# Masked MLP: transposes of the down product two groups ahead on three buffers, and search steps placed by duration

## The reference

```
x = x + attention(layernorm(x))          # 32 heads of 16, causal
x = x + ffn(layernorm(x))                # "f1"
x = x + masked_mlp(layernorm(x))         # "gates" and "down"
x = x + ffn(layernorm(x))                # "f2", same weights as f1

ffn:        down(silu(x @ gate) * (x @ up))         # 1792 wide, int weights dequantised
masked_mlp: s = silu(x @ w_gate.T)                  # 1376 wide
            s[the 688 smallest |s| of each row] = 0 # top_k(-abs(s), 688)
            (s * (x @ w_up.T)) @ w_down.T
```

## Time and profile before

| | us |
|---|---|
| median of three timed runs | 2203.8 |
| lowest and highest of them | 2194.07, 2206.63 |
| the profiled execution, its own time | 2189.01 |
| its span in the profile | 2187.2 |
| mean granted TensorE clock in it | 0.97 |

### The profile page before, as it was taken

How to read it: one execution, slowest core, us unless ns; L and a number is a source line. 1 busy time by engine, 2 the same in 40 slices (tenths; PEclk the granted TensorE clock), 3 DMA queues, 4 the chain that set the end, 5 groups by cost and what they waited for, 6 DMA issues and landing times.

```text
span 2187.2 us, 38402 instructions
## 1 busy us (share of the span) xinstructions
PE 2021.1 (92%) x14288; PEld 1234.7 (56%) x14288; DVE 1543.5 (71%) x2736; ACT 1022.0 (47%) x1658; POOL 558.7 (26%) x587
## 2 busy tenths in 40 slices
PE   5887999999999887899999999999999979889989
PEld 2342344444444345677677677677677555556656
DVE  6775677777777341289688597696696898989841
ACT  3221456656566521265364364373463564646511
POOL 2224354644342241012112012012012111121221
PEclk9997899999999988999999999999999999999999
DMA  7766234533233072110310400500400403031000
GB/s 258 236 220 175 67 99 117 139 88 83 76 84 93 19 244 110 55 50 1 108 49 1 154 23 1 175 1 1 174 2 14 152 1 132 24 113 53 11 11 10
DMA packets 115656, 187.35 MB, mean 86 GB/s; under 512 B 43200, under 2 KB 68176, under 8 KB 115520
## 3 DMA queue, kind: packets, MB, share of 16 engines
q1 hardware_dynamic: 91344, 133.22, 19.6%
q0 software_dynamic: 9088, 32.12, 5.1%
q10 hardware_dynamic: 15088, 20.19, 2.6%
HBM read 151.59 MB, written 33.62 MB: 85 GB/s over the span
## 4 chain that ended last, share of the span: by engine, by line
PE 46%; DVE 12%; issue 3%; ACT 1%; POOL 0%; DVEq 0%; ACTq 0%; POOLq 0%
PE ga L1364 10%; PE acc L1374 10%; PE ub L1364 10%; DVE junk L1534 7%; PE ga L1392 5%; PE ub L1392 5%; PE acc L1417 4%; DVE pat L1538 2%; DVE h L1591 1%; PE d_tr L1213 1%; DVE T L1540 1%; DVE lohi L1606 1%; PE d_tr L1403 0%; DVE X L1616 0%; DVE d_xn L1200 0%
## 5 line engine op out<-in xcount | busy, mean ns | idle before, releaser
L842 DVE TENSOR_REDUCE mx<-s 128x1 f32<-128x512 f32 (+3 forms) x608 | 380.8, 661 | 125.7 <-PE s L731 72.3
L1465 ACT ACTIVATE junk_a<-ax,T 128x1376 f16<-128x1376 f32 x248 | 357.8, 1443 | 200.8 <-DVE T L1540 195.1
L823 ACT ACTIVATE pr<-s 128x1024 f32<-128x1024 f32 (+3 forms) x352 | 301.2, 869 | 240.3 <-PE s L750 178.4
L1534 DVE TENSOR_SCALAR_CACHE_REDUCE junk<-ax,T 128x1376 f16<-128x1376 f32 x248 | 406.8, 1640 | 3.5
L1326 POOL TENSOR_TENSOR lohi<-h,lohi 128x256 f16<-128x256 f32 x224 | 172.7, 771 | 871.9 <-ACT lohi L1476 871.5
L1364 PE MATMUL ga<-xT_f,w_gate 128*128 128x256 f16 x2688 | 336.3, 276 | 38.4 <-DVE h L1591 35.3
L1364 PE MATMUL ub<-xT_f,w_up 128*128 128x256 f16 x2688 | 333.1, 274 | 0.0
L1364 PEld LDWEIGHTS ga<-xT_f,w_gate 128*128 128x128 f16 x2688 | 261.8, 99 | 121.1 <-DVE h L1591 54.7
L1374 PE MATMUL acc<-w_down,lohi 128*128 128x512 f16 x1344 | 326.1, 379 | 2.8 <-DVE X L1616 2.8
L1364 PEld LDWEIGHTS ub<-xT_f,w_up 128*128 128x128 f16 x2688 | 264.9, 99 | 32.4
L728 PE MATMUL s<-K,Q 65*128 65x512 f16 (+3 forms) x768 | 244.8, 344 | 26.0 <-DMA K<-onerow 12.9
(11 more groups left out here) (142 smaller groups left out, 2407.2 us busy)
## 6 DMA issues: line engine op xcount, KB each, us to landing
ring<-wgu_scr SPq DMA_DIRECT2D x64, 688.0 KB, 5.0
ring<-wd_scr SPq DMA_DIRECT2D x24, 768.0 KB, 4.7
wgu_scr<-tk_h POOLq DMA_DIRECT2D x16, 344.0 KB, 6.1
q_scr<-qk_h ACTq DMA_DIRECT2D x16, 256.0 KB, 4.0
k_scr<-qk_h ACTq DMA_DIRECT2D x16, 256.0 KB, 2.5
v_scr<-v_f ACTq DMA_DIRECT2D x16, 256.0 KB, 3.5
Q<-q_scr SPq DMA_DIRECT2D x32, 128.0 KB
K<-k_scr SPq DMA_DIRECT2D x32, 128.0 KB
```

What stands on the lines that cost most here:

```text
L823: nc.scalar.activation(pr[:, kb % 2, j0:j1, 0:w], scores, ACT.Exp, scale=SCALE).then_inc(e2_ok, 1)
L842: nc.vector.tensor_reduce(dst, s1[u % 2][:, 0:(j1 - j0) * w].rearrange("p (j k) -> p j k", k=w), AX.X, ALU.max).then_inc(r1_ok, 1)
L1465: nc.scalar.activation(junk_a[:, :], ax[k % 2][:, 1, :], ACT.Sign, scale=-1.0, bias=TF[:, 1:2], accum_out=cnt[:, 1:2]).then_inc(c1_ok, 1)
L1534: nc.vector.tensor_scalar(junk[:, :], ax[k % 2][:, 0, :], TF[:, 0:1], -float(KZERO), ALU.is_lt, ALU.add, accum_out=cnt[:, 0:1]).then_inc(c ...
```

## The change

Four edits, all in `phase_mlp` and `mlp_stages`:

1. `lohi` has NDT = 3 buffers in place of two; `hT` still uses the first two, `dT` all three. High and low halves and the product index `dT` by v % 3, and the high copy of group v waits for product v-3 in place of v-2.
2. TensorE's order in a down stage is turn 0, turn 1, then for each slot n: wait for low half n, turn n+2, product n. The wait for the low half stands ahead of turn n+2.
3. `junk_a` is removed. The sign pass writes its elementwise output into `kept[1]`, and the first sign pass of a chunk waits for both masks of the chunk before.
4. The items are placed by duration: `costs` gives each item its VectorE time, `evictions` and the terms beside it give VectorE's other work in a slot, and an item goes into a slot as long as the work done so far stays within the same share of all work as the time passed has of all time.

```diff
@@ phase_mlp @@
+    NDT = 3
...
-        lohi = [sb(f"lohi{i}", [P, 2 * DB * P], F16) for i in range(2)]
-        hT = [b[:, 0:2 * CW].rearrange("p (a n) -> p a n", a=2) for b in lohi]
+        lohi = [sb(f"lohi{i}", [P, 2 * DB * P], F16) for i in range(NDT)]
+        hT = [b[:, 0:2 * CW].rearrange("p (a n) -> p a n", a=2) for b in lohi[0:2]]
...
-        junk_a = sb("junk_a", [P, I_TK], F16)
...
@@ product_tk @@
-                pe.wait_ge(dl_ok, DU * k + v + 1)
...
-                        m = nc.tensor.matmul(acc[t][:, :], dT[v % 2][0:w, a, n, :], wr[:, b, :],
+                        m = nc.tensor.matmul(acc[t][:, :], dT[v % NDT][0:w, a, n, :], wr[:, b, :],
@@ TensorE's program @@
                     turn(s, 0)
+                    turn(s, 1)
                     if left:
...
-                        if n + 1 < DU:
-                            turn(s, n + 1)
+                        pe.wait_ge(dl_ok, DU * s.c + n + 1)
+                        if n + 2 < DU:
+                            turn(s, n + 2)
                         product_tk(s, n)
@@ signs, on ScalarE @@
                     act.wait_ge(t0_ok, k + 1)
+                    wait(act, hm_ok, TPC * k)
                 wait(act, p_ok, NBITS * k + i)
-                nc.scalar.activation(junk_a[:, :], ax[k % 2][:, 1, :], ACT.Sign, scale=-1.0, bias=TF[:, 1:2],
+                nc.scalar.activation(kept[1][:, :], ax[k % 2][:, 1, :], ACT.Sign, scale=-1.0, bias=TF[:, 1:2],
@@ turned, on ScalarE (turned_low on VectorE likewise indexes dT by v % NDT) @@
-                wait(act, dm_ok, DU * s.c + v - 1)
+                wait(act, dm_ok, DU * s.c + v - NDT + 1)
@@ mlp_stages @@
     spans = {"f1": 3860, "f2": 3860, "gates": 3460, "down": 1800}
+    evictions = {"f1": 430, "f2": 430, "gates": 530, "down": 460}
+    costs = [2450] * N_BITS + [80, 1740, 150, 950, 3180, 1650, 1900, 250, 250, 1740, 150, 150, 1740, 150, 950, 3180,
+                               1650, 1900]
     for k in range(NC):
         first = at["gates", k] + 1
-        own = [(slot, spans[s.kind]) for s in stages[first:at["down", k]] for slot in s.slots][:-2]
-        total = sum(span for _slot, span in own)
-        item = passed = 0
-        for slot, span in own:
+        own = [(slot, spans[s.kind], evictions[s.kind] + 700 * len(slot.taken) + 1800 * len(slot.stats)
+                + 1100 * len(slot.scaled) + 1400 * len(slot.lows))
+               for s in stages[first:at["down", k]] for slot in s.slots][:-2]
+        length = sum(span for _slot, span, _duty in own)
+        work = sum(duty for _slot, _span, duty in own) + sum(costs)
+        item = passed = done = 0
+        for slot, span, duty in own:
             passed += span
-            share = (N_BITS + FIN) * passed // total
-            slot.items += [(k, n) for n in range(item, share)]
-            item = share
+            done += duty
+            while item < len(costs) and (done + costs[item] // 2) * length <= passed * work:
+                slot.items.append((k, item))
+                done += costs[item]
+                item += 1
+        own[-1][0].items += [(k, n) for n in range(item, len(costs))]
     return stages
```

More of the change, by code:

```diff
@@ L1493, in turned @@
                     act.wait_ge(dn_ok, JB * s.ffns_done)
-                wait(act, dm_ok, DU * s.c + v - 1)
+                wait(act, dm_ok, DU * s.c + v - NDT + 1)
                 for rows, n0, n1_ in split_rows(v % DG):
-                    m = nc.scalar.activation(dT[v % 2][0:rows, 0, n0:n1_, :], tr[v % 2][0:rows, n0:n1_, :], ACT.Copy)
+                    m = nc.scalar.activation(dT[v % NDT][0:rows, 0, n0:n1_, :], tr[v % 2][0:rows, n0:n1_, :], ACT.Copy)
                     m.then_inc(dh_ok, 1)
@@ L1605, in turned_low @@
                 for rows, n0, n1_ in split_rows(v % DG):
-                    m = nc.vector.tensor_tensor(dT[v % 2][0:rows, 1, n0:n1_, :], tr[v % 2][0:rows, n0:n1_, :],
-                                                dT[v % 2][0:rows, 0, n0:n1_, :], ALU.subtract)
+                    m = nc.vector.tensor_tensor(dT[v % NDT][0:rows, 1, n0:n1_, :], tr[v % 2][0:rows, n0:n1_, :],
+                                                dT[v % NDT][0:rows, 0, n0:n1_, :], ALU.subtract)
                 m.then_inc(dl_ok, 1)
```

## The result

| | before | after |
|---|---|---|
| median of 13 runs, us | 2194.07 | 2182.07 |
| lowest and highest, us | 2186.63, 2207.63 | 2173.55, 2193.10 |
| span of the profiled execution, us | 2187.2 | 2172.5 |

The ratio of after to before is 0.9927, with a 95% interval of 0.9903 to 0.9951: the change makes the kernel 0.7% faster, 16 us of 2194 (11 to 21). The two medians are 12.0 us apart, which lies inside that interval too. The forecast was 15.8 us of 2189. As an absolute number it was 2188.0 us, 6 us above the median measured: with 13 runs in place of three, the median of the kernel before came down from 2203.8 to 2194.07.

What follows compares the result with a forecast made beforehand. TensorE bounds steady rounds; rounds of chunks 5 and 6 are bound by VectorE in one stage, TensorE in the next. Savings 2.0 + 5.9 + 3.7 + 4.2 = 15.8 us take 2203.8 to 2188.0 us, range 2172 to 2203.

Steps and rivals of the forecast that it cites:

- Part 1: Down stages: transposes two groups ahead leave the 1.62 us pause before product 0; net 0 per round.
- the slack: Between down slots, the new order gives VectorE one product more of room; credited with nothing.
- The mask wait: Downs 5 and 6: the first sign pass waits for GpSimd's mask, costing 1.1 us each, bounds 0 and 2.8.
- Round of chunk 5: Of VectorE's 11.9 us of waits 4.5 remain, 7.4 are saved; less 1.5 of collisions, net 5.9 us saved.
- The collisions of the pattern: Search's pattern instruction meeting GpSimd's low half takes 0.72 us, not 0.23; about 3 more in chunk 5's round, 1.5 us.
- Round of chunk 6: VectorE waits of 10.8 us, less 4.5 remaining, 1.5 of collisions and 1.1 of mask wait: 3.7 us saved.
- Round of chunk 7: TensorE's 5.9 us of waits for h and X go; down 6 costs 1.7; net 4.2 us saved.
- Round of chunk 0: TensorE's 2.0 us wait for X goes, as one step instead of two stands ahead of the addition.
- (a): Rival: VectorE's waits in rounds 5 and 6 reappear at down-stage ends and behind masks; 2197.6 us, chance 0.20.
- (b): Rival: the pause at each down start goes too, 11.3 us more saved; 2176.7 us, chance 0.05.
- (c): Rival: many pauses of about 1 us in f1 7 and f2 4 lower TensorE's clock; slower, 2229 us, chance 0.06.
- (d): Rival: nothing changes, as VectorE's total fixes the rounds and the rest is noise; 2203.8 us, chance 0.05.

Runs made afterwards that it cites:

- runs 5 to 7: The changed kernel with GpSimd's low half made to wait (2163.15 us), with a search step moved into the preceding down stage (2171.17), and with both (2170.66).
- run 5: The changed kernel with GpSimd's low half waiting, in slots holding only search steps, until the first step sets its next trial; 2163.15 us, ratio 0.9875.
- run 2: The kernel before with only the placement by duration; old order, two buffers and own scratch tile kept; 2179.34 us, ratio 0.9894.
- runs 1 and 2: The kernel before with everything but the new placement (2190.37 us, ratio 0.9953), and with the new placement alone (2179.34 us, 0.9894).
- Run 3: The kernel before with the new placement, old order, and the sign pass writing kept[1] behind the mask wait; 2175.17 us, ratio 0.9892.

## Why the prediction was right, point by point

**The bound.** Steady rounds bound by TensorE, rounds 5 and 6 by VectorE's work and idle time: runs 5 to 7 show it directly. The pattern instructions of these two rounds took 4.84 and 4.75 us more than their 0.229 us each in the changed kernel; with that gone in run 5 the rounds shortened by 4.8 and 4.7, and the steady ones kept their length.

**Part 1, costed at 0.** The pause of 1.62 us stayed, for the reason given. Off by size: a steady down lost 0.29 us. The trace of the kernel before shows where it stood. In a steady down the low halves of groups 5 and 7 each come right behind a search step:

```profile
1568.32 0.55 DVE L1606 TENSOR_TENSOR lohi<-d_tr,lohi 128x384 f16<-128x384 f32 x1
1568.46 0.49 PE L1403 MATMUL d_tr<-ident,pp 128*128 128x128 f32 x3
...
1568.93 2.12 PE L1417 MATMUL acc<-ring,lohi 128*128 128x512 f16 x9
...
1572.67 0.48 DVE L1606 TENSOR_TENSOR lohi<-d_tr,lohi 128x128 f16<-128x128 f32 x2
1573.20 0.98 PEld L1417 LDWEIGHTS acc<-ring,lohi 128*128 128x128 f16 x6 [0.48 <-DVE lohi L1606]
```

Product 5 starts 0.47 us after the transposes ahead of it, as its low half ends (1568.87), where 0.33 is usual. Product 7 loads its weights as its low half ends (1573.15), and the next stage starts 3.41 us after product 6 in place of the 3.24 of run 2. That is 0.14 + 0.17 us, each too short for a bracket on TensorE's matmuls. The order removes it because these groups are transposed one slot earlier, the placement because no step stands right ahead of these two; runs 1 and 2 agree. So the step that I had mis-sized is the slack: I gave nothing for it because where VectorE is late "it is the bound anyway", and it was late in steady downs too. In downs 4 to 6 the order gave 1.0 us in all where I gave nothing.

**The mask wait, 1.1 us twice.** Run 3 measured 0.79 and 0.78. The mechanism was the forecast one. In down 5 of the changed kernel VectorE took 2.1 us from the end of step 48 to its own first count, not 1.7: I had left out 0.53 us in which it waits for ScalarE's high copy of the group.

**Round of chunk 5, -5.9.** Down 4, f1 7 and gates 6 changed by -1.22 - 8.44 + 4.69 = -4.97 us. The gates' waits fell to 0, where I had left 0.5. Two things were mis-sized, and with them the sum comes to 4.7. The waits that remain are 5.0 us, not 4.5: the idle time at the first h is 3.87 us where I had 3.2, since VectorE is done earlier in the down stage but TensorE's last products and block 0 still follow. And a small instruction of the next layer norm met the new place of the first mask in gates 6, at 0.95 us where the same one took 0.17 on average before:

```profile
1814.91 2.79 POOL L1331 TENSOR_TENSOR pp<-pp,kept 128x1376 f32<-128x1376 f32 x1 [11.69 <-DVE kept L1586]
...
1816.79 0.95 DVE L1194 TENSOR_SCALAR rstd_f<-mv_f 128x2 f32<-128x2 f32 x1
```

The collisions of the pattern in this round were sized right. Its group from 1732.2 to 1804 us:

```profile
L1540 DVE TENSOR_SCALAR pat<-cnt,pow 128x2 int32<-128x2 f32 x25 | 10.6, 423 | 0.9
```

(10.6 - 25 x 0.229) / 0.49 = 10 of 25, three more than the 7 of before; in both traces the durations one by one give the same counts.

**Round of chunk 6, -3.7.** Measured -0.39 - 7.83 + 4.70 = -3.52.

**Round of chunk 7, -4.2.** The FFN stages lost 6.0 us against the 5.9 put down, down 6 gained 0.63 where I had 1.7. At 19.77 us it is 1.3 above the 18.46 of an undisturbed one, but the kernel before had lost 0.7 there already, which I had left out. Not foreseen was a loss at the end: TensorE waits twice for GpSimd's low halves.

```profile
2076.22 1.47 PE L1374 MATMUL acc<-w_down,lohi 128*128 128x512 f16 x6 [0.60 <-POOL lohi L1326]
...
2083.14 2.76 PE L1374 MATMUL acc<-w_down,lohi 128*128 128x512 f16 x12 [0.89 <-POOL lohi L1326]
```

The first pause lies in f2 6. It stands behind a low half of 2.87 us, where one that meets nobody takes 0.67; VectorE's scan (L1581) ran beside it:

```profile
2072.68 3.01 DVE L1581 TENSOR_TENSOR_SCAN kept<-junk 128x1376 f16<-128x1376 f16 x1
...
2073.30 2.87 POOL L1326 TENSOR_TENSOR lohi<-h,lohi 128x256 f16<-128x256 f32 x1 [4.52 <-ACT lohi L1478]
```

The second lies in down 7: there GpSimd does the last two low halves behind the second mask of chunk 7, which ends at 2082.46. Down 7 took 27.97 and 28.01 us in the two kernels with the old placement and 28.75 to 29.80 in the eight with the new one, so its 0.78 us are a cost of the placement. f2 7 varies from 61.0 to 62.4 us in the ten profiles, so its 0.45 us are not to be told from chance.

**Round of chunk 0, -2.0.** Measured -3.63: the pause for X of 2.0 us went, and two small ones for h, 0.6 us, which I had left out. That is 2.6; the stages had been 3.59 us longer than the steady pair's 108.82. The rest is in the distances between starts. The 12 matmuls ahead of the pause for X start 3.47 us before what follows them, where 1.31 is usual: 2.16 us, not 2.00, because a group's duration of 1.46 to 1.47 reaches over the start of the next one and a pause counts only from its end. The two pauses for h cost 0.87 us in the same way, and three more of 0.19 each are too short for the list. Together 3.6 us.

**The sum.** -15.8 forecast, -17.7 in the stages, -16 by the ratio. The savings put too low (round 0, the steady downs) and too high (round 5) partly cancel, so it is in part luck that the total came this close.

**The rivals.** (a) fell: the gates' waits did not come back elsewhere; the gates' 4.7 us are TensorE waiting for a full VectorE, which was in the sum. (b) fell: the pause is the same. (c) fell: pauses of 1.02 us in a row, up to 1.75, left f1 7 at a granted clock of 1.00. What the Trainium skill describes in "TensorE: Matmul & The Clock Gate", section "A second HAM failure mode: psum-queue depth-cycling", did not appear in this trace: short idling between the groups did not make the clock swing. The longer pauses are gone too. In the kernel before, one of 2.23 us in f2 4 was followed by the low level, as those of 3.24 us were, and one of the same length in f1 7 was not:

```profile
1752.86 1.48 PE L1364 MATMUL ga<-xT_f,w_gate 128*128 128x256 f16 x12 [2.23 <-DVE h L1591]
```

```profile
1877.16 2.74 PE L1364 MATMUL ga<-xT_f,w_gate 128*128 128x256 f16 x12 [2.23 <-DVE h L1591]
```

(d) fell with the interval.

## What to carry to other kernels

Where one engine's side work is spread over another's slots, cost it by duration and fill all slots of the round alike, but ask first which rounds that engine bounds: the same edit was worth 0.3 us in a round of 159 us and 3.5 to 5 us in one of 120. What such a round pays is the sum of that engine's work and idle time, so its waits at the stage borders and its collisions with other engines are worth more than the order of the engine that everyone watches. A tile shared to save room brings a wait; price it against what the room buys (1.6 us given, 1.0 us gained in the downs concerned).

## What the runs showed of the hardware

A VectorE instruction of two elements per partition takes 0.23 us alone. In the changed kernel 124 of the 248 took 0.44 to 0.72 us, 46.4 us more in all, and every one of the 124 ended about 0.02 us after a subtraction of GpSimd that ran beside it; in the kernel before it was 91, 44.6 us in all. VectorE's 1.64 us counting pass kept its time beside the same GpSimd instruction (1639 ns on average in the page above). Spacing the elements 32 bytes apart changed nothing; one wait on GpSimd removed them all.

The pattern instruction is not the only one. A subtraction of one value per partition (L1558), 0.15 us alone, took 2.72 us in five of the eight chunks of the changed kernel, until GpSimd's mask ended:

```profile
1683.05 2.79 POOL L1331 TENSOR_TENSOR pp<-pp,kept 128x1376 f32<-128x1376 f32 x1
1683.14 2.72 DVE L1558 TENSOR_TENSOR step<-succ,T 128x1 f32<-128x1 f32 x1
```

In the rounds of chunks 5 and 6 it took 0.19 us, so it cost these nothing. And it is not always VectorE that waits: GpSimd's low half of 2.87 us beside the scan, above, is the other case. No run here tried to move these two.
